# Behind two sparse layers, the weighted sum and the norm are spread over ScalarE, GpSimd and VectorE

## What is computed

```
def _layernorm(x, axis=-1, eps=1e-05):
    m = jnp.mean(x, axis=axis, keepdims=True)
    v = jnp.var(x, axis=axis, keepdims=True)
    return (x - m) / jnp.sqrt(v + eps)
...
    x = x + _L2_xattn_ref(_layernorm(x, axis=-1), ctx_1024, ...)   # E2: relu experts
    x = x + _L2_ffn_ref(_layernorm(x, axis=-1), ...)               # E3: silu(gate) * up experts
    x = x + _L3_xattn_ref(_layernorm(x, axis=-1), ctx_1024, ...)   # A3: attention, 16 heads
```

## Time and profile before

| | |
|---|---|
| median of 3 runs | 997.4 us (996.21 to 999.2) |
| profiled execution | 998.37 us |
| its span (first to last instruction) | 996.5 us |
| busy: TensorE, weight loads | 783.5 us, 646.9 us |
| busy: VectorE, ScalarE, GpSimd | 651.3 us, 468.0 us, 371.2 us |
| granted TensorE clock, mean | 0.875 |

### The profile page before, as it was taken

One profiled execution on the slowest core, in us unless ns is written; L12 is line 12 of the kernel. 1 busy time (PEld: TensorE's weight loads), 2 busy tenths in 40 slices (PEclk: granted clock), 3 DMA queues, 4 the chain that ended last, 5 costly groups with the idle time before them and its releaser, 6 DMA issues.

```text
span 996.5 us, 24233 instructions
## 1 busy us (share of the span) xinstructions
PE 783.5 (79%) x8057; PEld 646.9 (65%) x8057; DVE 651.3 (65%) x1641; ACT 468.0 (47%) x948; POOL 371.2 (37%) x470
## 2 busy tenths in 40 slices
PE   6998889999999879998299983479893499849005
PEld 3776788888888668996298872379883266633005
DVE  3886765777777677776655336633334699967895
ACT  3786425544555244443066541046562166615753
POOL 5663602111110080110367772047773466310800
PEclk9999698999999969999699996569997599958557
DMA  6300000000000000004434224011214000000001
GB/s 190 97 0 1 1 1 2 2 3 1 0 0 2 1 1 22 20 18 144 125 95 115 76 48 114 21 30 52 53 52 108 1 3 0 1 0 0 0 0 43
DMA packets 49218, 36.06 MB, mean 36 GB/s; under 512 B 7665, under 2 KB 44978, under 8 KB 49138
## 3 DMA queue, kind: packets, MB, share of 16 engines
q1 hardware_dynamic: 43420, 24.45, 8.7%
q0 software_dynamic: 4992, 10.23, 3.8%
q10 hardware_dynamic: 726, 0.33, 0.1%
HBM read 26.73 MB, written 8.26 MB: 35 GB/s over the span
## 4 chain that ended last, share of the span: by engine, by line
PE 55%; DVE 18%; POOL 11%; issue 7%; ACT 4%; DMA 3%; DVEq 1%; ACTq 1%; SPq 0%; POOLq 0%
PE psum L1140 7%; POOL y_scratch L1903 5%; POOL E_rows L1895 5%; PE psum L738 3%; PE psum L680 3%; PE psum L643 3%; PE psum L1781 3%; PE psum L658 3%; PE psum L373 2%; PE psum L2078 2%; PE psum L347 2%; PE psum L317 2%; DVE X L1986 2%; PE psum L1109 2%; PE psum L1806 2%
## 5 line engine op out<-in xcount | busy, mean ns | idle before, releaser
L1781 PE MATMUL psum<-E_XT,E_weights 128*128 128x128 f32 x780 | 104.1, 282 | 1.5 <-DVE E_XT L1931 0.8
L1781 PEld LDWEIGHTS psum<-E_XT,E_weights 128*128 128x128 f32 x780 | 96.9, 198 | 2.9 <-DVE E_XT L1931 1.5
L1895 POOL DMA_INDIRECT E_rows<-rows_scratch,route_token_of x78 | 76.5, 981 | 58.0 <-DVE route_token_of L1614 29.9
L1903 POOL DMA_INDIRECT y_scratch<-E_y,route_place_of x78 | 77.9, 998 | 32.5 <-issue 20.7
L1397 DVE SCALAR_TENSOR_TENSOR X<-psum,E_gates,X 128x128 f32<-128x128 f32 x256 | 71.8, 344 | 26.3 <-PE psum L1140 25.9
L493 POOL TENSOR_TENSOR A_kexp<-A_kT,hmask 128x512 f32<-128x512 f32 x64 | 66.4, 1058 | 27.6 <-ACT A_kT L414 27.6
L1140 PEld LDWEIGHTS psum<-E_w,E_h 128*128 128x128 f32 x512 | 67.9, 194 | 11.4 <-ACT E_h L1226 5.9
L1226 ACT ACTIVATE E_h<-psum,cols 128x512 f32<-128x512 f32 x64 | 43.8, 687 | 61.5 <-PE psum L1111 61.5
L1140 PE MATMUL psum<-E_w,E_h 128*128 128x128 f32 x512 | 68.8, 278 | 4.6 <-ACT E_h L1226 3.9
L198 POOL TENSOR_TENSOR rstd<-vareps,nhalf 128x4 f32<-128x4 f32 x24 | 24.7, 1031 | 124.1 <-DVE vareps L192 124.1
L1862 ACT ACTIVATE E_h<-psum,cols 128x128 f32<-128x128 f32 x156 | 44.5, 368 | 55.4 <-PE psum L1781 55.4
(11 more groups left out here) (320 smaller groups left out, 2133.5 us busy)
## 6 DMA issues: line engine op xcount, KB each, us to landing
routed_back<-y_scratch SPq DMA_DIRECT2D x16, 256.0 KB, 4.6
E_first<-in_L_xattn_W SPq DMA_DIRECT2D x1, 2048.0 KB, 8.9
L1w<-in_L_xattn_W SPq DMA_DIRECT2D x8, 256.0 KB, 4.6
rows_scratch<-xn SPq DMA_DIRECT2D x8, 256.0 KB, 2.3
E_w<-in_L_ffn_routed_w SPq DMA_DIRECT2D x28, 64.0 KB, 1.8
E_raw<-in_L_ffn_w_down SPq DMA_DIRECT2D x8, 176.0 KB
E_rows<-rows_scratch,route_token_of POOLq DMA_INDIRECT x78, 2.9
y_scratch<-E_y,route_place_of POOLq DMA_INDIRECT x78, 2.3
```

Of the source, the lines that this page charges most:

```text
L1781: mm = pe.matmul(out[:, c * P:(c + 1) * P], WE[:, p, (k0 + c) * P:(k0 + c + 1) * P], XT[:, p, :], start=True, stop=True)
L1895: pool.indirect_dma_start(out=xg[:, i % 4, :], out_offset=None, in_=rows[:, :], in_offset=bass.IndirectOffsetOnAxis(ap=disp.token_of[:, i: ...
L1903: pool.indirect_dma_start(out=yrows[:, :], in_=y[:, i % 3, :], in_offset=None, out_offset=bass.IndirectOffsetOnAxis(ap=disp.place_of[:, i: ...
```

## The change

E2 and E3 share the code, so the change takes effect twice: behind E2 (with E3's norm) and behind E3 (with A3's norm).

- ScalarE multiplies the second choices by their gates, in place in `back[:, 1]`: four activations (Copy with a scale per partition) per group, as soon as the group has landed.
- GpSimd adds the whole group to X in one operation of 128x512.
- VectorE then adds the first choices with their gates (four operations per group), and computes mean, variance + eps, and now also -mean (`moments`).
- GpSimd computes rstd as before and then shift = -mean * rstd (`shift`).
- ScalarE applies the norm, xn = rstd * X + shift: four activations per group (Identity with scale and bias per partition).
- ScalarE's evacuations of the next layer's turns are now written in the same loop; the late preparation stands at the end of E2 instead of the start of E3.

```
+class NormSpread(NormAll):
...
+    def moments(self, dve, g):
...
+        self.stats(dve, g)
+        dve.tensor_scalar(m.minus_mean[:, ts], m.meanvar[:, ts, 0], -1.0, None, ALU.mult).then_inc(self.minus_mean_ready.sem, 1)
+
+    def shift(self, pool, g):
...
+        self.rstd(pool, g)
+        pool.wait_ge(*self.rstd_ready(g + 1))
+        pool.wait_ge(*self.minus_mean_ready(g + 1))
+        pool.tensor_tensor(m.shift[:, ts], m.minus_mean[:, ts], m.rstd[:, ts], ALU.mult).then_inc(self.shift_ready.sem, 1)
+
+    def apply_by_scalar(self, act, g):
+        m = self.m
+        act.wait_ge(*self.shift_ready(g + 1))
+        for t in range(g * GT, (g + 1) * GT):
+            ap = act.activation(m.xn[:, t, :], m.X[:, t, :], ACT.Identity, bias=m.shift[:, t:t + 1], scale=m.rstd[:, t:t + 1])
+        ap.then_inc(self.xn_ready.sem, 1)
...
     def scalar(act):                      (of dispatched_experts, at its end)
+        if spec.get("late"):
+            spec["late"].scalar(act)
+        act.wait_ge(*disp.gate_ready(1))
+        after = m.norm_after[tag]
+        for g in range(NG + 2):
+            if g < NG:
+                act.wait_ge(*y_here[g](32))
+                for t in range(g * GT, (g + 1) * GT):
+                    ac = act.activation(back[:, 1, t, :], back[:, 1, t, :], ACT.Copy, scale=disp.gate[:, 1, t:t + 1])
+                ac.then_inc(weighed.sem, 1)
+            if 0 <= g - 2:
+                after.evacuate(act, g - 2)
+            if 0 <= g - 1 < NG:
+                after.apply_by_scalar(act, g - 1)
...
     def gpsimd(pool):                     (at its end)
+        after = m.norm_after[tag]
+        for g in range(NG + 1):
+            if g < NG:
+                ts = slice(g * GT, (g + 1) * GT)
+                pool.wait_ge(*weighed(g + 1))
+                pool.tensor_tensor(m.X[:, ts, :], m.X[:, ts, :], back[:, 1, ts, :], ALU.add).then_inc(added.sem, 1)
+            if g:
+                after.shift(pool, g - 1)
...
     def vector(dve):                      (at its end)
         for g in range(NG):
             dve.wait_ge(*y_here[g](32))
-            for k in range(2):
-                if k:
-                    dve.wait_ge(*taken(g * GT + GT))
-                for t in range(g * GT, (g + 1) * GT):
-                    st = dve.scalar_tensor_tensor(out=m.X[:, t, :], in0=back[:, k, t, :], scalar=disp.gate[:, k, t:t + 1],
-                                                  in1=m.X[:, t, :], op0=ALU.mult, op1=ALU.add)
-                    if k == 0:
-                        st.then_inc(taken.sem, 1)
+            dve.wait_ge(*added(g + 1))
+            for t in range(g * GT, (g + 1) * GT):
+                st = dve.scalar_tensor_tensor(out=m.X[:, t, :], in0=back[:, 0, t, :], scalar=disp.gate[:, 0, t:t + 1],
+                                              in1=m.X[:, t, :], op0=ALU.mult, op1=ALU.add)
             st.then_inc(combined.sem, 1)
             dve.wait_ge(*combined(g + 1))
-            after.stats(dve, g)
-            if g:
-                after.apply(dve, g - 1)
+            after.moments(dve, g)
```

More of the change, by code:

```diff
@@ L245, in sb @@
             return scope.enter_context(nc.sbuf_tensor(f"{tag}_{name}", shape, dt))
-        norm = NormAll(sh, m, None) if early else Norm(sh, sb, f"{tag}_ln", m)
+        norm = NormSpread(sh, m) if early else Norm(sh, sb, f"{tag}_ln", m)
         if not early:
@@ L405, in scalar @@
     def scalar(act):
-        if early:
-            for g in range(NG):
-                norm.evacuate(act, g)
         m.begin(act, start)
@@ L468, in gpsimd @@
         if early:
-            for g in range(NG):
-                norm.rstd(pool, g)
-        if early:
             m.begin(pool, start)
@@ L511, in vector @@
     def vector(dve):
-        if early:
-            norm.apply(dve, NG - 1)
         m.begin(dve, start)
@@ L1712, in dispatched_experts @@
             turns.begin(sb("raw", [P, 2, 3, 3 * P]), spec["turn_from"], m.banks[5], m.ident[:, :])
-    norm = NormAll(sh, m, None) if gated else NormRows(sh, m)
+    norm = NormSpread(sh, m) if gated else NormRows(sh, m)
     xn_ready = norm.xn_ready
@@ L1730, in dispatched_experts @@
     y_here = [signal(f"routed_y_here{g}", 32) for g in range(NG)]
-    taken, combined = signal("routed_first_taken", NT), signal("routed_combined", NG)
+    weighed, added, combined = signal("routed_second_weighed", NG), signal("routed_second_added", NG), signal("routed_combined", NG)
     L.done = combined(NG)
@@ L1757, in tensor @@
     def tensor(pe):
-        if spec.get("late"):
-            spec["late"].tensor(pe)
         if gated:
@@ L1820, in tensor @@
         second(NTILE - 1)
+        if spec.get("late"):
+            spec["late"].tensor(pe)
         if spec.get("then_attention"):
@@ L1825, in scalar @@
     def scalar(act):
-        if spec.get("late"):
-            spec["late"].scalar(act)
         if gated:
-            for g in range(NG):
-                norm.evacuate(act, g)
             disp.table(act, J1)
@@ L1881, in scalar @@
                     turns.keep(act, turned_at(i))
+        if spec.get("late"):
+            spec["late"].scalar(act)
[11 more added lines that the diff above has]
+                after.apply_by_scalar(act, g - 1)
     def gpsimd(pool):
-        for g in range(NG):
-            norm.rstd(pool, g)
+        if not gated:
+            for g in range(NG):
+                norm.rstd(pool, g)
         m.begin(pool, start)
@@ L1913, in gpsimd @@
                 send(i - 2)
+        after = m.norm_after[tag]
+        for g in range(NG + 1):
+            if g < NG:
+                ts = slice(g * GT, (g + 1) * GT)
+                pool.wait_ge(*weighed(g + 1))
+                pool.tensor_tensor(m.X[:, ts, :], m.X[:, ts, :], back[:, 1, ts, :], ALU.add).then_inc(added.sem, 1)
+            if g:
+                after.shift(pool, g - 1)
     def vector(dve):
-        norm.apply(dve, NG - 1)
+        if not gated:
+            norm.apply(dve, NG - 1)
         if gated:
@@ L2361, in build @@
         m.vareps, m.rstd = sb("vareps", [P, NT]), sb("rstd", [P, NT])
+        m.minus_mean, m.shift = sb("minus_mean", [P, NT]), sb("shift", [P, NT])
         m.ident = sb("ident", [P, P])
@@ L2519, in build @@
         makers[4] = lambda st: dispatched_experts(sh, m, "E2", st, dict(
-            E=8, C=4, func=ACT.Relu, dispatch=m.dispatch, prepare=late.vector, b1=b1_2, b2all=b2all,
+            E=8, C=4, func=ACT.Relu, dispatch=m.dispatch, late=late, prepare=late.vector, b1=b1_2, b2all=b2all,
             w1=e2_first, w2=e2_last, weights_here=e2_here(16 * 9), back=m.back, turns=m.turns,
@@ L2523, in build @@
         makers[5] = lambda st: dispatched_experts(sh, m, "E3", st, dict(
-            E=8, C=3, gated=True, dispatch=m.dispatch3, late=late, wr=wr3, then_attention=6 in which,
+            E=8, C=3, gated=True, dispatch=m.dispatch3, wr=wr3, then_attention=6 in which,
             w1=m.turns.first, w2=m.turns.last, weights_here=m.turns.ready(3 * 8), back=m.back))
```

7 lines of the change are left out of this document (added).

## The result

Measured beside each other, the kernel before takes 998.27 us (996.21 to 999.76, five runs) and the changed one 1005.57 us (1000.81 to 1008.44, five runs): a ratio of 1.006, with a 95% interval of 1.0038 to 1.0082, so slower by 4 to 8 us. A later repeat, with twelve runs of the changed kernel, gave 1003.93 us and 1.0045 (1.0022 to 1.0068). The forecast was slower by 4.3 us. Its absolute time was low: 1005.57 lies 0.8 us above the range's end, and the repeat's 1003.93 inside it.

The account below looks back on a forecast made before the run. Two serial stretches behind E2 and E3, paced by VectorE's 4.77 us period, were taken to bound what the change touches. 998.37 + 1.4 + 2.9 = 1002.7 us, less 1.0 for the median: 1001.7, range 997.2 to 1004.8.

Parts of the forecast that it names:

- What bounds the stretches: Behind E2 and E3: both stretches are serial, so what they gain or lose reaches the end one to one.
- Landing and the first weighing, add: Behind E2: landing unchanged at 606.30; weighing 1.26, add 1.27 and hand-overs put VectorE's first choices at 609.02.
- Variance of group 0: Behind E2: first choices to end of variance take 2.67 us as before, so variance is there at 611.69.
- the landing of the later groups hides: Behind E2: later groups' transfers land before they are needed, group 1's at 608.4, group 3's at 612.4, needed at 620.
- The ring: Both stretches: apply, weigh, add, power, shift and hand-overs run in series per group, 5.55 us against 4.77.
- rival 1: Both stretches: ScalarE's activation groups cost only 1.14 us each, so no difference, 997.5 us; chance 0.18.
- Third turn: TensorE's third turn starts 1.4 us later behind E2, at 625.87 instead of 624.48, and the same behind E3.
- Fourth turn behind E3: Application 3 stands behind evacuation 2 on ScalarE: 3.36 us between the turns instead of 1.90, +1.5 us more.
- Sum: Whole kernel: +1.4 us behind E2 and +2.9 behind E3, 4.3 us slower; chance 0.60.
- 2: Both stretches: GpSimd is held up at every add, 2.0 us each; paths lose 3.6 and 5.0, 1006.0 us; chance 0.10.
- 4: The loss does not arrive, because a DMA or the routing has unseen slack: 998 to 999 us; chance 0.06.
- rival 3: Both stretches: a free pointer and an add of 1.04 us would gain 3.2 and 2.4, 991.8 us; chance 0.06.

Follow-up runs that it names:

- e4: The changed kernel with ScalarE's application leaving out the shift by the mean, so one pointer fewer; one run, 1000.58 us.
- e3: Against the kernel before, only the sum is moved: ScalarE weighs all groups first, GpSimd adds, the norm stays on VectorE; ratio 0.9938.
- r3: The kernel of e3 run once more, unchanged, for a second trace; ratio to the kernel before 0.9974.
- e1: The changed kernel with ScalarE weighing all four groups before it applies anything; ratio to the kernel before 0.9966.
- e6: Against the kernel before: behind E2 only the norm moved; behind E3 the change's division, all weighings first, applications ahead of preceding evacuations; 992.27 us, ratio 0.9925.
- the filler: The changed kernel with 150 unread identity products on TensorE behind E3, while it would wait, to keep its clock up; ratio to the kernel before 1.0125.

## Why the prediction was right, point by point

- **What bounds the stretches.** Right: both are serial, and what they lose arrives at their ends. What the two traces of the change show beyond them doesn't repeat (the attention lasted 107.24 and 104.42 us). The edits without a price cost nothing: the late preparation's last activation ends 4.1 us ahead of the first weighing, where it ended 4.3 us ahead of VectorE's start, and ScalarE has nine table loads in both traces.
- **Landing and the first weighing, add.** Right: from start to VectorE's first choices 606.77 - 604.00 = 2.77 us, against 2.72.
- **Variance of group 0.** Missed by 0.4 us, and in its place. The prediction had the collision of add(1) with VectorE's first choices, at 0.2 us, and left it to the range. Group 1 landed later (weigh(1) at 607.16, 3.16 us behind the start, where the prediction had 608.4 - 606.30 = 2.1), so the add met the variance instead (timeline behind E2, after):

```profile
607.16 1.28 ACT L1909 ACTIVATE routed_back<-routed_back,route_gate 128x128 f32<-128x128 f32 x4 [1.87 <-DMA routed_back<-y_scratch]
...
608.51 1.26 POOL L1953 TENSOR_TENSOR X<-X,routed_back 128x512 f32<-128x512 f32 x1 [1.88 <-ACT routed_back L1909]
...
609.26 0.54 DVE L192 TENSOR_SCALAR vareps<-meanvar 128x4 f32<-128x4 f32 x1
```

  0.54 us instead of 0.17, and it ends with the add (609.80 and 609.77). In the other traces the time goes with the landing: with weigh(1) 2.5 to 2.7 us behind the first weighing the variance + eps takes 0.17 us, with 2.96 us 0.33 (e4), with 3.12 us 0.49 and with 3.32 us 0.71 (the repeat, behind E2 and E3). The step that went wrong is the sentence that the landing of the later groups hides: for the path it does, but it sets what runs beside what. The rule of the Trainium skill that the prediction weighed ("GPSIMD Engine Reference", "Key points") names two SBUF inputs or a 2-port mode on VectorE's side. The pairs of e3 and r3 agree with it, since VectorE's operation has two inputs in SBUF there. The row held here, L192, has one input of 128x4 and a constant; that it contends is seen, but whether it runs in a 2-port mode no row shows.
- **The ring.** Right: 5.50 and 5.49 us (applications at 611.23, 616.73, 622.22) against 5.55. Prices against the forecast: application 1.65 (1.65), weighing 1.26 (1.26), add 1.26 (1.27), power 1.01 to 1.04, once 1.16 (1.03), shift 0.20 to 0.25 (0.24). Pricing the activations by the rows with the same number of pointers, rather than by the 157 nearer at hand, is what decided against rival 1. The ring in the timeline behind E2, after:

```profile
611.23 1.65 ACT L259 ACTIVATE xn<-X,shift,rstd 128x128 f32<-128x128 f32 x4 [2.80 <-POOL shift L253]
...
615.50 1.14 DVE L2027 SCALAR_TENSOR_TENSOR X<-routed_back,route_gate,X 128x128 f32<-128x128 f32 x4 [2.89 <-POOL X L1953]
...
616.73 1.65 ACT L259 ACTIVATE xn<-X,shift,rstd 128x128 f32<-128x128 f32 x4 [1.99 <-POOL shift L253]
```

- **Third turn.** +1.73 behind E2 and +1.45 behind E3, against +1.4.
- **Fourth turn behind E3.** Right in mechanism, +1.63 against +1.5; the turn came 0.24 us behind the application, not 0.04.
- **Sum.** +4.8 us in the first trace and +5.2 in the repeat against +4.3; the collision is most of the difference: 0.4 us behind E2 in the first trace, 0.3 and 0.5 in the repeat.
- **The absolute time.** The forecast stood on a median of 997.4 us; before's later medians were 998.3 to 1000.1. Neither this nor the 5 us to either side over which one kernel's runs spread was in the range, which is why the first median fell outside though the ratio is right.
- **Rivals.** 1 fell by the activations' prices, 2 because VectorE does wait during adds 2 and 3 (idle 2.89 us before L2027, released by L1953) and the adds keep to 1.26 us; its price of 2 us for a held add was right, as r3's 2.09 shows. 4 fell because the stretches' loss arrives. 3, faster, needed a ring of 4.5 us. The runs show that this side was there, but by another way than rival 3's cheaper operations: e1 takes the weighing out of the ring at unchanged prices, and is faster than before.

What stays open: why TensorE's clock rises 7 us into the attention in one execution and 20 in another of nearly the same work; what sets the 10 us by which executions differ ahead of the first stretch; and about 1.7 us of e6's gain beyond its stretches, which is no more than that spread.

## What to carry to other kernels

When work is spread over several engines, draw the cycle that one group's work makes through the queues and add it up: it is the cycle, not the busiest engine, that sets the period. An operation that needs nothing from the cycle (here the weighing, ready since the landing) must not stand behind one that does. The same operations took 1.0045 to 1.006 of the time before in one order and 0.9966 of it in another; and leaving the sum where it was and moving only the norm (0.9945) took fewer hand-overs for as much gain.

## What the runs showed of the hardware

- GpSimd and VectorE hold each other up when both work on tiles in SBUF, and either may be the one that waits, even with the same offset (0.16 and 0.17 us) between their starts: VectorE's four operations with two inputs 2.14 us instead of 1.14, its 128x4 operation 0.54 and 0.71 instead of 0.17, GpSimd's 128x512 add 2.09 instead of 1.26. In the pairs with L2027 the two together took 2.1 to 2.3 us, nearly the sum of both alone.
- Whether they meet can depend on when transfers land: in the traces that have the change's operations, the 128x4 operation took 0.17 us with group 1's weighing 2.5 to 2.7 us behind the first, and 0.71 us with 3.32.
- An activation over 128 columns from SBUF to SBUF takes 388 ns with one pointer and 482 with two; in a row of four they start 0.29 and 0.39 us apart.
- TensorE's clock doesn't stay up for having been up: at 1.00 (2.4 GHz) through the filler, which ended at 792.2, it was at 0.50 (1.2 GHz) from 797 on, with the engine busy 0.60 us of the 3 from 792 to 795. With the rise 12.5 us into the attention this took 104.42 us, with the rise after 7 us 104.55, and with the rise after 20 us 107.24.
